# Two diagonal key steps of the softmax sums move from TensorE to VectorE, and the sum over keys moves three slots back

## The chip, the cores and the metric

The kernel runs on one core of a Trainium2 chip, as one launch. The metric is the device time of a run in microseconds (us). The cores that are not used do nothing. TensorE does the matmuls, ScalarE the exponentials and many copies out of PSUM, VectorE the row maxima and the small statistics, GpSimd long additions over SBUF tiles, SyncE issues the DMAs.

## What is computed

The input is two sequences of 2048 tokens with 1024 features. The layer is multi-query attention (32 heads of 32 features, one key and one value head) between two normalizations, and then a feed-forward of eight low-rank adapters mixed by a router, again between two normalizations, with a residual each time. Cut to what matters:

```python
q = (x @ wq).reshape(B, T, 32, 32); k = x @ wk; v = x @ wv
scores = einsum('bqhd,bkd->bhqk', q, k) * scale
scores = where(causal, scores, -inf)
out = einsum('bhqk,bkd->bqhd', softmax(scores), v).reshape(B, T, C) @ wo
x = x + layernorm(out)            # attention of layernorm(x)
x = x + layernorm(router_lora(layernorm(x)))
```

The change concerns the denominator of the softmax: for every query and head, the sum of the exponentials over all keys that the query may see.

## The kernel before

The queries are cut into blocks of 512 (four per sequence, eight in all), and each block into eight **units** of four heads. There are 64 units, n = 0 to 63; `n % 8` is the unit's place in its block, and the block's place in its sequence, `qb_of(n)`, says how many keys it sees. A unit goes over the keys in **steps** of 128: 4, 8, 12 or 16 steps for blocks 0 to 3. The last four steps of a unit lie on the diagonal: there only 512, 384, 256 and 128 of the queries see the keys, and the tiles are that wide. A **slot** is one head of one step, so a unit has 16, 32, 48 or 64 slots. Everything is set in order by slots: `pieces` (L139) lists, for each engine and each slot of a unit, the extra work that stands there, and every engine walks through the same slots in its own program.

In a slot TensorE computes the scores of one head and step (L1493, into a bank of PSUM), ScalarE takes their exponential into the tile `pr` (L834, one of three step buffers), and TensorE computes a block of scores for a later unit (L1481), of which VectorE takes the maximum over keys (L1086), so that the shift of the exponentials is known in time. The order in which scores and maxima take PSUM is one ring of five banks (L314, L1459): whoever comes next in TensorE's order takes the bank that was taken five places before, and waits until its reader is done. With one maximum per slot, the scores of slot j take the bank of the maximum of slot j-3.

When the four heads of a step are exponentiated, TensorE multiplies them with the values (L1517, four matmuls of 32 columns side by side, accumulated in one bank over the whole unit). This set stands a few slots later, beside the scores of the next step.

The **denominators** come together on two engines. For most steps GpSimd adds the four heads' tiles of the step to a running sum `ds` (L730: a step of full width is one instruction of 2048 elements per partition; the step 0 is added with step 1). At the end of a unit TensorE sums `ds` over the keys with a matmul by ones (`sum_keys`, L1557, in the list as "sums"). The steps that `by_pe` (L57) names are not added by GpSimd: TensorE multiplies their tiles by ones directly (L1542), right behind the values of that step, into the same bank that the sums then complete. In units of 12 steps these are the four diagonal steps 8 to 11, in units of 16 steps 12 to 15 (10 to 15 in the last two units of a block). GpSimd also masks the diagonal corner of each diagonal step (`mask`, L747).

After the sums ScalarE takes a first guess of the reciprocal (a logarithm and an exponential, "guess", L844), VectorE refines it in two operations (L1113) and scales the values with it (L1124). For units whose sums TensorE has begun itself, "sums" stands at slot 2 of the next unit, and the guess, the refinement and the scaling at slots 3 to 7. TensorE delays a piece to the next slot where the values stand and a projection is in front of it (`beside_values`, L200).

GpSimd's first addition of the next unit waits for the sums (`den_ready`), since it overwrites `ds`. An exponential that overwrites a step buffer waits for the values of three steps before and, where GpSimd adds that step, for its addition.

Beside this, the units carry the projections of other blocks, the residuals and the normalizations: VectorE's statistics of the attention's output (`att`, L1187), GpSimd's residual (L755: a scaling at L760 that needs VectorE's inverse root, and an addition at L762), GpSimd's normalization of the next block's tokens (L764) and its last residual sum of the layer (L769).

## Time and profile before

| | |
|---|---|
| median of 3 runs | 3328.93 us (3324.53 to 3332.82) |
| the profiled execution, its own time | 3326.88 us |
| its span, first to last instruction | 3325.1 us |
| TensorE busy | 96% |
| VectorE, GpSimd, ScalarE busy | 65%, 62%, 50% |
| mean granted TensorE clock | 0.986 |

The page of the profile gives shares of the span, the chain of work that ended last, and groups of instructions by line. Matmuls overlap, and their ends are modelled: the length of a set of matmuls is read from its start to the start of what follows it on TensorE, not from its own duration. A group "PEld" is the loading of weights, which runs beside the matmul before it; a load that waits costs time only where no matmul runs beside it. GpSimd is called POOL and VectorE DVE in the rows. Stretches are read from the table of windows, which gives each engine's busy time between two moments.

### The profile page before, as it was taken

Reading aid. Unit: us, or ns where it says so; the run is one execution under the profiler, and the core shown is the slowest. Engines: PE = TensorE matmul, PEld = TensorE weight load, DVE = VectorE, ACT = ScalarE, POOL = GpSimd, SP = SyncE. Lnnn points to the kernel's source line nnn. Section 1 sums busy time; section 2 is a strip of 40 time slices with the busy share of each in tenths; the row PEclk is TensorE's granted clock in tenths of the full one; section 3 lists DMA queues with packets and bytes.
Section 4 is the critical chain, followed back from the end, with each engine's and each line's share of the span. In section 5 each row is a group of like instructions: output and inputs, shape, how many; then the busy total and the mean of one; then the engine's idle time right before and its main releaser. Section 6 shows DMA issues by size and latency. Waiting matters only on the chain.

```text
span 3325.1 us, 45565 instructions
## 1 busy us (share of the span) xinstructions
PE 3191.2 (96%) x15976; PEld 1606.5 (48%) x15976; DVE 2163.1 (65%) x5848; ACT 1661.8 (50%) x3306; POOL 2061.2 (62%) x741
## 2 busy tenths in 40 slices
PE   7899999999999999999999999999999999999997
PEld 3444554455554455554444445544555444554444
DVE  4666677767767667774365667676776776677605
ACT  2334555555555555555433345545555554555552
POOL 1335676776676888777311176677576677778870
PEclk9999999999999999999999999999999999999998
DMA  4422111201101001101211211111010100011000
GB/s 118 116 61 65 52 52 39 61 26 30 52 23 58 23 23 30 29 23 39 64 52 52 81 45 40 42 44 60 26 56 23 39 17 23 26 43 48 7 1 26
DMA packets 133012, 144.04 MB, mean 43 GB/s; under 512 B 28200, under 2 KB 93736, under 8 KB 132784
## 3 DMA queue, kind: packets, MB, share of 16 engines
q1 hardware_dynamic: 132480, 140.72, 14.4%
q8 instruction: 127, 2.08, 0.3%
q14 instruction: 101, 0.83, 0.1%
q10 hardware_dynamic: 304, 0.41, 0.0%
HBM read 72.91 MB, written 16.78 MB: 27 GB/s over the span
## 4 chain that ended last, share of the span: by engine, by line
PE 73%; POOL 15%; DVE 5%; ACT 3%; issue 3%; SPq 1%; DMA 1%; POOLq 0%; ACTq 0%; DVEq 0%
PE ps L1501 14%; PE ps L1529 12%; PE ps L1490 12%; POOL ds L745 12%; PE ps L1632 11%; PE ps L1455 10%; PE ps L1542 3%; POOL ds L742 2%; PE ps L1591 2%; PE ps L1672 1%; ACT pr L842 1%; PE ps L1686 1%; PE ps L1564 1%; SPq L637 1%; PE ps L1642 1%
## 5 line engine op out<-in xcount | busy, mean ns | idle before, releaser
L842 ACT ACTIVATE pr<-ps 128x512 f32<-128x512 f32 (+3 forms) x2560 | 1299.8, 534 | 1303.0 <-PE ps L1501 885.0
L745 POOL TENSOR_TENSOR ds<-ds,pr 128x2048 f32<-128x2048 f32 (+1 forms) x360 | 1491.6, 4143 | 133.1 <-ACT pr L842 100.5
L1501 PE MATMUL ps<-qs,ks 98*128 98x512 f32 (+3 forms) x2560 | 1349.4, 534 | 22.4 <-ACT pr L842 6.7
L1095 DVE TENSOR_REDUCE mx<-ps 128x1 f32<-128x512 f32 x1536 | 1009.2, 685 | 389.7 <-PE ps L1490 381.7
L1490 PE MATMUL ps<-ks,qs 96*128 96x512 f32 (+3 forms) x2560 | 957.2, 385 | 51.6 <-ACT pr L842 28.8
L1501 PEld LDWEIGHTS ps<-qs,ks 98*128 98x128 f32 x2560 | 482.9, 190 | 763.7 <-issue 294.6
L1092 DVE CUSTOM_DVE_ANT_0 ps<-ps,mask_qk 128x128 f32<-128x128 f32 (+3 forms) x1024 | 498.4, 503 | 476.5 <-PE ps L1490 471.6
L1490 PEld LDWEIGHTS ps<-ks,qs 96*128 96x128 f32 x2560 | 486.7, 192 | 312.3 <-ACT pr L842 157.6
L1529 PE MATMUL ps<-pr,vs 128*32 128x512 f32 (+3 forms) x5120 | 612.0, 546 | 0.6 <-POOL pr L752 0.3
L1455 PE MATMUL ps<-xT,wq_sb 128*128 128x512 f32 x1024 | 513.7, 599 | 5.5 <-ACT zs L885 3.1
L1632 PE MATMUL ps<-wo_sb,ao 128*128 128x512 f32 x896 | 453.4, 598 | 0.5 <-DVE q L1084 0.5
L752 POOL TENSOR_SCALAR_AFFINE_SELECT pr<-pr 128x512 f32<-128x512 f32 x192 | 121.6, 634 | 464.6 <-ACT pr L842 464.6
L742 POOL TENSOR_TENSOR ds<-pr 128x2048 f32<-128x2048 f32 (+1 forms) x56 | 246.6, 4403 | 220.7 <-ACT pr L842 220.7
L1455 PEld LDWEIGHTS ps<-xT,wq_sb 128*128 128x128 f32 x1024 | 186.2, 192 | 82.6 <-issue 59.5
L1529 PEld LDWEIGHTS ps<-pr,vs 128*32 128x32 f32 x5120 | 102.8, 108 | 187.0 <-issue 155.6
L1632 PEld LDWEIGHTS ps<-wo_sb,ao 128*128 128x128 f32 x896 | 164.4, 191 | 57.7 <-issue 35.7
L1092 DVE DVE_READ_ACCUMULATOR2_ANT mx<- 128x1 f32 x1024 | 145.0, 142 | 0.0
L771 POOL TENSOR_TENSOR xr<-xr,zs 128x1024 f32<-128x1024 f32 x28 | 66.4, 2372 | 126.8 <-ACT zs L920 126.8
L1542 PE MATMUL ps<-pr,ones 128*32 128x512 f32 (+3 forms) x1344 | 129.8, 455 | 0.6 <-DVE ao L1127 0.6
L760 POOL TENSOR_SCALAR zs<-zs,r_att 128x1024 f32<-128x1024 f32 x28 | 31.2, 1114 | 131.4 <-DVE r_att L1049 131.4
L1084 DVE TENSOR_TENSOR q<-ps,q 128x512 fp32r<-128x512 f32 x64 | 44.2, 691 | 64.9 <-ACT q L826 64.9
L741 POOL COPY ds<-pr 128x512 f32<-128x512 f32 x8 | 4.9, 609 | 108.0 <-ACT pr L842 108.0
(166 smaller groups left out, 2105.7 us busy)
## 6 DMA issues: line engine op xcount, KB each, us to landing
qs<-q SPq DMA_DIRECT2D x762, 64.0 KB, 2.0
wq_sb<-in_L_attn_wq_dram SPq DMA_DIRECT2D x64, 512.0 KB, 4.0
t<-in_L_attn_x_dram SPq DMA_DIRECT2D x32, 512.0 KB, 6.3
xr<-in_L_attn_x_dram SPq DMA_DIRECT2D x28, 512.0 KB, 4.6
out_dram<-xr SPq DMA_DIRECT2D x28, 512.0 KB, 4.7
wo_sb<-in_L_attn_wo_dram SPq DMA_DIRECT2D x8, 512.0 KB, 5.2
qs<-mT SPq DMA_DIRECT2D x252, 4.0 KB
xT<-in_L_attn_x_dram SPq DMA_DIRECT2D x4, 512.0 KB, 5.5
```

The costliest lines, as they stand in the source:

```text
L742: nc.gpsimd.tensor_tensor(ds[:, :, c0:], first[:, :, c0:], this, ALU.add).then_inc(added, 1)
L745: nc.gpsimd.tensor_tensor(ds[:, :, c0:], ds[:, :, c0:], this, ALU.add).then_inc(added, 1)
L752: nc.gpsimd.affine_select(out=here, in_=here, compare_op=ALU.is_ge, fill=0.0, base=0, pattern=[[0, GH], [1, P]], channel_multiplier=-1).th ...
L842: nc.scalar.activation(pr[:, k % NS, g, c0:], ps[:, PM + EXP_PLACE[head(n, t, g)] % NPM, c0:], ACT.Exp, scale=SCALE).then_inc(exp_done, 1)
L1092: nc.vector.tensor_tensor_reduce(out=seen, in0=seen, in1=mask_qk[:, BLK - w:], op0=ALU.add, op1=ALU.max, scale=1.0, scalar=3.0 * NEG, accu ...
L1095: nc.vector.tensor_reduce(found, seen, AX.X, ALU.max).then_inc(mx_done, 1)
L1455: last = nc.tensor.matmul(ps[:, PX, :], wq_sb[:, n % NW, k, :], xT[:, k, :], start=(k == 0), stop=(k == KT - 1))
L1490: nc.tensor.matmul(ps[:, bank, 0:w], qs[0:STK, n % NS, g, qt * P:(qt + 1) * P], ks[0:STK, c:c + w], start=True, stop=True).then_inc(mx_rea ...
L1501: last = nc.tensor.matmul(ps[:, bank, c0:], ks[0:STK + 2, c:c + P], qs[0:STK + 2, n % NS, g, c0:], start=True, stop=not by_mask)
L1529: last = nc.tensor.matmul(ps[g * HD:(g + 1) * HD, PPV, c0:], vs[:, row, :], pr[:, (UNIT_STEP[n] + t) % NS, g, c0:], start=(t == 0), stop=( ...
L1542: last = nc.tensor.matmul(ps[g * HD:(g + 1) * HD, PAUX, c0:], ones[:, :], pr[:, (UNIT_STEP[n] + t) % NS, g, c0:], start=(t == by_pe(n)[0]) ...
L1632: last = nc.tensor.matmul(ps[:, PX, :], ao[:, (n + k) % NAO, j % TB * P:(j % TB + 1) * P], wo_sb[:, k, h * HALF:(h + 1) * HALF], start=(k ...
```

## The change

`by_pe` gives up the second and the third diagonal step in 30 units: in the sixteen of 12 steps (9 and 10, tiles of 384 and 256 columns) and in fourteen of the sixteen of 16 steps (13 and 14). The last unit of each sequence (n = 31 and 63) keeps what it had. A new function `hand_add` adds these steps on VectorE to GpSimd's running sum `ds`, one instruction per head, after GpSimd's last addition of the unit. A step's four adds stand two steps later in VectorE's program, one per slot behind that slot's maxima: for the first at the last four slots of the unit, for the second at slots 0 to 3 of the next. In these units the sums stand at slot 5 instead of 2, and the guess, the refinement and the scaling three slots later with them. ScalarE's exponential three steps on waits for the add of its head, and the sums wait for all adds of the unit.

```diff
     def by_pe(n):

+        if n % (NU * NQ) == NU * NQ - 1:
+            return (10, 11, 12, 13, 14, 15)
         if qb_of(n) == 3:
-            return (10, 11, 12, 13, 14, 15) if n % NU >= 6 else (12, 13, 14, 15)
-        return ((0, 1, 2, 3) if n >= NU else (), (), (8, 9, 10, 11), ())[qb_of(n)]
+            return (10, 11, 12, 15) if n % NU >= 6 else (12, 15)
+        return ((0, 1, 2, 3) if n >= NU else (), (), (8, 11), ())[qb_of(n)]
+
+    def by_dve(n):
+
+        return () if qb_of(n) < 2 or n % (NU * NQ) == NU * NQ - 1 else (TB * qb_of(n) + 1, TB * qb_of(n) + 2)
...
             if not whole(n - 1):
-                put(2 if by_pe(n - 1) else 6, "PE", "sums", n - 1)
-            first, apart = 3 if by_pe(n - 1) else 6 if N == 16 else 7, 2 if by_pe(n - 1) and N > 16 else 1
+                put(5 if by_dve(n - 1) else 2 if by_pe(n - 1) else 6, "PE", "sums", n - 1)
+            first, apart = 6 if by_dve(n - 1) else 3 if by_pe(n - 1) else 6 if N == 16 else 7, 2 if by_pe(n - 1) and N > 16 else 1
...
+        for m in range(max(n - 1, 0), n + 1):
+            for t in by_dve(m):
+                for g in range(GH):
+                    j = GH * (t + 2) + g - (slots(m) if m < n else 0)
+                    if 0 <= j < N:
+                        put(j, "DVE", "hand", m, t, g)
...
+                if k >= NS and step_of(k - NS)[1] in by_dve(step_of(k - NS)[0]):
+                    act.wait_ge(dve_added, hands_to(*step_of(k - NS), g))
                 act.wait_ge(st_ready, head(n, t, g) + 1)
...
+            def hand_add(n, t, g):
+
+                c0, _ = cols(n, t)
+                dve.wait_ge(added, UNIT_ADD[n + 1])
+                if t > by_dve(n)[0]:
+                    dve.wait_ge(dve_added, hands_to(n, t - 1, g))
+                dve.wait_ge(exp_done, head(n, t, g) + 1)
+                dve.wait_ge(masked, masks_to(n, t))
+                nc.vector.tensor_tensor(ds[:, g, c0:], ds[:, g, c0:], pr[:, (UNIT_STEP[n] + t) % NS, g, c0:],
+                                        ALU.add).then_inc(dve_added, 1)
...
             def sum_keys(n):
                 pe.wait_ge(added, UNIT_ADD[n + 1])
+                if by_dve(n):
+                    pe.wait_ge(dve_added, UNIT_HAND[n + 1])
```

How the instructions move is shown at the boundary from unit 26 to unit 27 (16 steps each). In these rows `ps<-qs,ks` are scores, `ps<-ks,qs` the blocks for the maxima, `pr,vs` values, `pr,ones` a step's sums on TensorE, `ds,ones` the sums over keys, `wo_sb,ao` projections. Line numbers of the changed kernel are higher, since lines were put in.

TensorE in the last slot of unit 26, before:

```order
L1490 MATMUL ps<-ks,qs 128x512
L1529 MATMUL ps<-pr,vs 32x256 x4
L1542 MATMUL ps<-pr,ones 32x256 x4
L1501 MATMUL ps<-qs,ks 128x512
L1490 MATMUL ps<-ks,qs 128x512
L1632 MATMUL ps<-wo_sb,ao 128x512
```

The same place in the change:

```order
L1524 MATMUL ps<-ks,qs 128x512
L1563 MATMUL ps<-pr,vs 32x256 x4
L1535 MATMUL ps<-qs,ks 128x512
L1524 MATMUL ps<-ks,qs 128x512
L1668 MATMUL ps<-wo_sb,ao 128x512
```

The set of step 14 is gone; the set of step 13 is gone in the same way four slots earlier.

TensorE from the values of the last step on, slots 2 and 3 of unit 27, before:

```order
L1529 MATMUL ps<-pr,vs 32x128 x4
L1542 MATMUL ps<-pr,ones 32x128 x4
L1501 MATMUL ps<-qs,ks 128x512
L1490 MATMUL ps<-ks,qs 128x512
L1632 MATMUL ps<-wo_sb,ao 128x512
L1564 MATMUL ps<-ds,ones 32x512 x4
```

In the change, from the projection of slot 3 on:

```order
L1668 MATMUL ps<-wo_sb,ao 128x512
L1535 MATMUL ps<-qs,ks 128x512
L1524 MATMUL ps<-ks,qs 128x512
L1535 MATMUL ps<-qs,ks 128x512
L1524 MATMUL ps<-ks,qs 128x512
L1563 MATMUL ps<-pr,vs 32x512 x4
L1535 MATMUL ps<-qs,ks 128x512
L1524 MATMUL ps<-ks,qs 128x512
L1668 MATMUL ps<-wo_sb,ao 128x512
L1600 MATMUL ps<-ds,ones 32x512 x4
```

The sums went from slot 3 to slot 6, each time behind a projection; the set of step 15 stays. In 16 of the 30 boundaries they end up at slot 6 like this, in the others at slot 5.

VectorE at the same boundary, slots 60 to 63 and 0, before (maxima are `mx<-ps`):

```order
L1048 TENSOR_SCALAR a_pre<-y_pre,w_pre 128x1
L1049 TENSOR_SCALAR r_pre<-a_pre,y_pre 128x1
L1148 TENSOR_SCALAR nb<-mv_pre,r_pre 128x1
L1095 TENSOR_REDUCE mx<-ps 128x1 x4
L1016 BN_STATS st_att<-zs 128x6
L1021 BN_AGGR mv_att<-st_att 128x2
L1095 TENSOR_REDUCE mx<-ps 128x1
```

In the change:

```order
L1180 TENSOR_SCALAR nb<-mv_pre,r_pre 128x1
L1142 TENSOR_TENSOR ds<-ds,pr 128x384
L1116 TENSOR_REDUCE mx<-ps 128x1
L1142 TENSOR_TENSOR ds<-ds,pr 128x384
L1116 TENSOR_REDUCE mx<-ps 128x1
L1142 TENSOR_TENSOR ds<-ds,pr 128x384
L1116 TENSOR_REDUCE mx<-ps 128x1
L1142 TENSOR_TENSOR ds<-ds,pr 128x384
L1116 TENSOR_REDUCE mx<-ps 128x1
L1037 BN_STATS st_att<-zs 128x6
L1042 BN_AGGR mv_att<-st_att 128x2
L1142 TENSOR_TENSOR ds<-ds,pr 128x256
```

Between each two maxima an add has come in; three more of 256 columns follow in slots 1 to 3, with the operations of the inverse root between them. GpSimd's and SyncE's programs keep their order.

## Rows read from the trace of the kernel before

**Rows 1.** The page: busy engines; the chain that ended last, by engine.
```profile
PE 3191.2 (96%) x15976; PEld 1606.5 (48%) x15976; DVE 2163.1 (65%) x5848; ACT 1661.8 (50%) x3306; POOL 2061.2 (62%) x741
...
PE 73%; POOL 15%; DVE 5%; ACT 3%; issue 3%; SPq 1%; DMA 1%; POOLq 0%; ACTq 0%; DVEq 0%
```

**Rows 2.** Windows: busy time of each engine at boundaries; the sum is over 28.
```profile
core 0: us, PE busy (x) PEld busy (x) DVE busy (x) ACT busy (x) POOL busy (x), PEclk, DMA share, GB/s
651.77:662.91 11.14, 11.05 (x78) 5.62 (x74) 7.17 (x15) 6.10 (x13) 1.82 (x2) 1.00 0.32 78
...
1268.70:1279.83 11.13, 11.13 (x79) 5.48 (x75) 8.65 (x24) 6.16 (x14) 4.30 (x4) 1.00 0.29 71
...
2758.78:2769.41 10.63, 10.54 (x77) 5.10 (x73) 6.53 (x11) 5.88 (x13) 0.63 (x1) 1.00 0.28 69
...
3054.14:3063.28 9.14, 9.14 (x74) 4.86 (x70) 7.39 (x18) 5.62 (x14) 2.99 (x2) 1.00 0.28 67
...
sum 306.18, PE 304.77 PEld 155.99 DVE 229.54 ACT 176.05 POOL 80.53; mean PE 10.88 PEld 5.57 DVE 8.20 ACT 6.29 POOL 2.88
...
1557.13:1573.13 16.00, 15.21 (x104) 6.57 (x100) 4.83 (x13) 11.50 (x25) 8.41 (x4) 1.00 0.32 83
```

**Rows 3.** Timeline of TensorE, boundary 26 to 27: start us, us, line, operation.
```profile
1267.94 0.83 PE L1542 MATMUL ps<-pr,ones 128*32 128x384 f32 x8
1268.70 0.33 PE L1501 MATMUL ps<-qs,ks 98*128 98x128 f32 x1
...
1271.57 0.61 PE L1542 MATMUL ps<-pr,ones 128*32 128x256 f32 x8
1272.12 0.50 PE L1501 MATMUL ps<-qs,ks 98*128 98x512 f32 x1
...
1275.74 1.02 PE L1632 MATMUL ps<-wo_sb,ao 128*128 128x512 f32 x2
1276.69 1.07 PE L1564 MATMUL ps<-ds,ones 128*32 128x512 f32 x8
1277.68 0.50 PE L1501 MATMUL ps<-qs,ks 98*128 98x512 f32 x1
```

**Rows 4.** Timeline of VectorE at the same boundary: maxima.
```profile
1269.34 0.69 DVE L1095 TENSOR_REDUCE mx<-ps 128x1 f32<-128x512 f32 x1 [1.27 <-PE ps L1490]
...
1270.63 1.88 DVE L1095 TENSOR_REDUCE mx<-ps 128x1 f32<-128x512 f32 x3
```

**Rows 5.** Whole span: waits of score loads (us, times, longest); idle of score matmuls.
```profile
PEld ps L1501 <- DVE mx L1095: 211.7, 352, 1.7
...
L1501 PE MATMUL ps<-qs,ks 98*128 98x512 f32 x1792 | 1001.7, 567 | 14.3 <-DMA qs<-mT 5.2 <-ACT pr L842 4.8 <-DVE mx L1095 2.3
```

**Rows 6.** VectorE: the add of two SBUF tiles (ns min/median/max); masked maxima by shape.
```profile
L1395 DVE TENSOR_TENSOR xT<-xT,t x6: 682/691/693, 3307.2 to 3321.8; 128x512 f32<-128x512 f32 x6
...
L1092 DVE CUSTOM_DVE_ANT_0 ps<-ps,mask_qk 128x512 f32<-128x512 f32 x256 | 177.1, 707 | 121.8 <-PE ps L1490 121.0
...
L1092 DVE CUSTOM_DVE_ANT_0 ps<-ps,mask_qk 128x384 f32<-128x384 f32 x256 | 141.7, 570 | 82.2 <-PE ps L1490 80.3
L1092 DVE CUSTOM_DVE_ANT_0 ps<-ps,mask_qk 128x256 f32<-128x256 f32 x256 | 108.5, 434 | 149.2 <-PE ps L1490 147.8
```

**Rows 7.** Timeline of GpSimd at the same boundary.
```profile
1260.55 4.55 POOL L745 TENSOR_TENSOR ds<-ds,pr 128x2048 f32<-128x2048 f32 x1
...
1271.44 0.63 POOL L752 TENSOR_SCALAR_AFFINE_SELECT pr<-pr 128x512 f32<-128x512 f32 x1 [3.21 <-ACT pr L842]
1272.06 1.19 POOL L766 TENSOR_SCALAR t<-t,r_pre,nb 128x1024 f32<-128x1024 f32 x1
1273.22 2.38 POOL L771 TENSOR_TENSOR xr<-xr,zs 128x1024 f32<-128x1024 f32 x1
1279.69 1.11 POOL L760 TENSOR_SCALAR zs<-zs,r_att 128x1024 f32<-128x1024 f32 x1 [4.09 <-DVE r_att L1049]
...
1283.21 4.57 POOL L742 TENSOR_TENSOR ds<-pr 128x2048 f32<-128x2048 f32 x1
```

More of the change, by code:

```diff
@@ L67, in adds_in, with by_gpsimd @@
     def adds_in(n, t):
-        return sum(x not in by_pe(n) for x in range(1, max(t, 1) + 1))
+        return sum(by_gpsimd(n, x) for x in range(1, max(t, 1) + 1))
+    def by_gpsimd(n, t):
+        return t not in by_pe(n) and t not in by_dve(n)
     UNIT_STEP = [0]
     UNIT_ADD = [0]
+    UNIT_HAND = [0]
     for n_ in range(UN):
         UNIT_STEP.append(UNIT_STEP[-1] + steps(n_))
+        UNIT_HAND.append(UNIT_HAND[-1] + GH * len(by_dve(n_)))
         UNIT_ADD.append(UNIT_ADD[-1] + adds_in(n_, steps(n_) - 1))
@@ L455, in bass_mqa_sandwich_lora_router @@
         off_ready = sem("off_ready")
+        dve_added = sem("dve_added")
         ao_ready = sem("ao_ready")
@@ L607, in masks_to, with hands_to @@
             return TB * (n - n // NU // NQ * NU - NU) + t - TB * qb_of(n) + 1
-        def by_gpsimd(n, t):
-            return t not in by_pe(n)
+        def hands_to(n, t, g):
+            return UNIT_HAND[n] + GH * by_dve(n).index(t) + g + 1
         def turn_bank(j, h):
@@ L1276, in _ @@
                     for stage, *a in at.get(j, []):
-                        if stage == "refine":
+                        if stage == "hand":
+                            hand_add(*a)
+                        elif stage == "refine":
                             refine(*a)
```

## Prediction

> **What bounds the kernel now.** I read the page first: TensorE is busy 96% of the span, and most of the chain that ended last is TensorE's own lines, with a part that passes through GpSimd's sums [rows 1]. So a matmul set taken from TensorE is worth its length, unless something else then ends last where it stood. The question is asked per unit boundary, because every removed set and every added VectorE instruction lies there: in the last four slots of a 12- or 16-step unit (44 to 47, or 60 to 63) and the first four of the next (0' to 3'). I call the stretch from the scores of the fourth-last slot to the scores of slot 6' a boundary; the change touches 30 of them (16 of 12-step units, 14 of 16-step units).
>
> The table of windows gives TensorE and VectorE there [rows 2]. TensorE is at full clock and busy for nearly all of each (304.77 of 306.18 us in 28 of them). VectorE is far from the 65% of the page: 8.65 of 11.13 us, 7.17 of 11.14, 7.39 of 9.14. Over the 28 it idles 306.18 - 229.54 = 76.64 us, 2.74 a boundary. Only behind the two units that are followed by little work for the maxima does it idle over 11 us (16.00 - 4.83 in one).
>
> The timelines of one boundary (26 to 27 of the first batch) show how the queues run [rows 3, 4]. What ties them is the ring of five banks: the scores of slot j take the bank that the maximum of slot j-3 left, where a slot has one maximum. So TensorE can be three slots ahead of VectorE, no more, and loads for scores do wait for a maximum, 211.7 us in 352 waits, nearly all of it behind a matmul that still streams: the matmuls themselves stood idle for it for 2.3 us [rows 5]. VectorE's chain starts 0.64 us behind the first scores (1268.70 to 1269.34), when the first maximum is there. Maxima in a row take 0.60 each (three in 1.88, one lasting 0.69).
>
> **What the change removes.** Two sets of ones-matmuls a boundary: 384 wide, 1267.94 to the next instruction at 1268.70, 0.76 us; 256 wide, 1271.57 to 1272.12, 0.55 us [rows 3]. That is 1.31 us, 39.3 us in 30. The sums of the keys (1276.69 to 1277.68) stay whole and move later; so do the two logarithm and exponential steps on ScalarE and the refinement and scaling on VectorE, without changing their work. They cost nothing by being later: the next user of that bank on TensorE is far down the unit. GpSimd's first addition of the next unit waits for the sums, but it needs the exponentials of slot 7' too, which come behind them; were the sums later than that, this addition would be next to be late.
>
> **What it adds.** Eight additions on VectorE a boundary, four of 384 and four of 256 columns, each reading both operands from SBUF. The one such instruction in the trace is 512 wide: 0.691 us [rows 6]. The masked maximum falls by 0.137 us with each 128 columns (0.707, 0.570, 0.434), so 0.555 and 0.418. Overlapped as maxima are (0.09), they hold the queue 0.46 and 0.33: 4 x 0.46 + 4 x 0.33 = 3.16 us a boundary. Their own waits, for GpSimd's last addition and for exponentials, are over by then: the addition ended at 1265.10 [rows 7], the first VectorE add comes after 1269. ScalarE's new wait, an exponential three steps on waiting for the add in its slot, ends before TensorE's: the maximum queued behind that add releases the scores three slots later.
>
> **The queue without collisions.** VectorE now has a continuous chain: 0.64 us start, all its work, the adds, and then the sums (1.0 us), during which it catches up with what was in the window behind slot 3'. The boundary then lasts its length less the idle time plus 3.16 + 0.64 = 3.80 us. With the 0.76 us saved ahead of it, a boundary changes by 3.04 us less its VectorE idle time: it breaks even at 3.04, and the mean is 2.74. For 28 boundaries: 28 x 3.04 - 76.64 = +8.5 us. In 16 of the 30 the sums come out at slot 6', behind a projection pair. There the scores of slot 6' wait for the maximum of slot 3' alone, not for the add (0.33) and small operations (up to 0.45) behind it, while the pair ahead of the sums costs 0.95 us where 0.46 is usual (1275.74 to 1276.69) [rows 3]; I credit 0.45 each, -7.2 us. The two with idle VectorE keep the whole saving, -2.6. Sum: -1.3 us. The queue gives back nearly all that TensorE gains.
>
> **Collisions with GpSimd.** In these slots GpSimd runs a mask (0.63 us), in 12 boundaries a normalization (1.19) and in 16 a residual sum (2.38) right behind it [rows 7]. All read SBUF, as both operands of the new adds do. What such an add does beside a running GpSimd instruction, the trace does not show: VectorE's instructions there read PSUM or one SBUF operand, and the adds of [rows 6] ran while GpSimd was idle. The lower end is nothing (0 us). The upper end is that an add waits until the running instruction has ended. An add comes about every 1.06 us (maximum 0.60, add 0.46), so it meets an instruction on average 0.53 us after its start: a residual sum costs 2.38 - 0.53 = 1.85, a normalization 0.66, a mask 0.63 x 0.63 / (2 x 1.06) = 0.19. In four 12-step boundaries the residual sum falls on some 1.3 us of statistics and small operations, and 0.55 is left. Sum: 12 x 1.85 + 4 x 0.55 + 12 x 0.66 + 28 x 0.19 = 37.6 us. In such a chain a wait is not made up: the maxima queue behind it, and TensorE is three slots from them. No row is near this case; that both operands come from the memory in which GpSimd's instruction works, while every VectorE instruction that ran beside GpSimd undisturbed had one there at most, makes me take the upper end, and keep both.
>
> The Trainium skill, page "SBUF — State Buffer", section "Who interferes with whom", says that a VectorE instruction with two SBUF inputs and a GpSimd instruction that reads SBUF shut each other out, the later one for the whole of the earlier. By that the sum is the upper end, without it the lower. No row of this trace shows it.
>
> **Sum.** The profiled execution took 3326.88 us (its span 3325.1), 2.05 below the median of the three runs. 3326.88 - 1.3 + 37.6 = 3363.2 us: **slower by 1.1%**.
>
> **Rivals.** (1) No collisions, the queue alone: 3326.88 - 1.3 = 3325.6, no change. For it: no row shows an instruction of either engine held up by the other. Its bounds: if every semaphore wait at the chain's end costs 0.3 us more, +9; if slots 4' to 6' take up half of the adds, -15. (2) The adds vanish in VectorE's idle time, because TensorE's lead of three slots (some 3 us) covers the whole of the 3.16 us and is rebuilt before the next boundary: then the removed sets count in full, 3326.88 - 39.3 = 3287.6, or about 3307 if half does. This is the other side. It decides where the idle time of a boundary is over 4.35 us (3.04 + 1.31); only 2 of 30 are, and 3 more come near (3.97 twice and 4.10 us [rows 2]), which speaks against it. (3) Collisions, and late statistics on top: the root that GpSimd's residual waits for (to 1279.69 [rows 7]) is behind the adds in VectorE's queue. In 10 boundaries the next unit's first GpSimd addition follows that residual at once, as at 1283.21; 1 us more in each gives 3373.
>
> **How the numbers follow.** About 0.3% (10 us) is what a measurement of this kernel can tell from no change. Collisions, with or without (3): 0.61, of it 0.58 slower by more than that and 0.03 where few adds meet an instruction. Rival 1: 0.24, of it 0.16 the same, 0.04 on either side. Rival 2: 0.15, of it 0.14 faster. That makes faster 0.18, same 0.20, slower 0.62. The range goes from 3314, which leaves out most of rival 2, to 3380 (rival 3 with some of the waits doubled); about 0.18 lies outside. The likeliest case alone has 3345 to 3380.
>
> **What would show it.** In the changed profile TensorE has 60 sets fewer (480 matmuls) and VectorE 240 adds. If I am right, TensorE's loads for scores wait more for VectorE, some adds last or wait until the end of a residual sum or normalization, and boundaries with a residual sum grow by 1.5 to 3 us while those with a mask alone stay within 1 us. If the adds run at 0.56 and 0.42 us straight through a residual sum, rival 1 is right. If boundaries shrink by 1.3 us each, rival 2 is. A chain that ends through GpSimd's first additions more than before speaks for rival 3. A change of more than 1 us outside the boundaries would show that I looked in the wrong place.

## The result and the profile after

The changed kernel takes 3403.98 us (3400.13 to 3408.60 in 4 runs), the kernel before, measured beside it, 3329.93. The ratio is 1.0223, with a 95% interval of 1.0209 to 1.0237. I forecast slower by 1.1% with a range of 3314 to 3380 us. The direction was right; the time is 40.8 us over my forecast and outside the range.

The profiled execution took 3408.60 us (span 3406.9), so the two profiled executions differ by 81.7 us. Busy engines and chain on the page of the changed kernel:

```profile
PE 3226.3 (95%) x15496; PEld 1607.5 (47%) x15496; DVE 2293.8 (67%) x6088; ACT 1667.3 (49%) x3306; POOL 2071.5 (61%) x741
...
PE 70%; POOL 13%; DVE 9%; issue 3%; ACT 3%; SPq 1%; DMA 1%; DVEq 0%; POOLq 0%; ACTq 0%
```

TensorE has the 480 matmuls fewer (15976 to 15496) and is nevertheless busy 35 us longer, 3226.3 against 3191.2 [rows 1]. Fewer instructions take longer together: either each waits inside, or the clock is lower. VectorE's part of the chain went from 5% to 9%, so the wait for VectorE is there too.

The table of windows tells the two apart. The windows run from the scores of the fourth-last slot to the scores of slot 8', not 6' as in [rows 2], since the sums now stand as late as slot 6'. Before, boundary 26 to 27 and the sum over the same 28 boundaries; every one of the 28 has a granted clock of 1.00 there:

```profile
1268.70:1282.19 13.49, 13.49 (x86) 6.94 (x83) 11.01 (x28) 7.33 (x16) 6.58 (x5) 1.00 0.40 103
...
sum 358.53, PE 356.95 PEld 190.78 DVE 278.79 ACT 206.56 POOL 111.50; mean PE 12.75 PEld 6.81 DVE 9.96 ACT 7.38 POOL 3.98
```

After, the boundaries behind units 17, 22, 26 and 29, and the sum:

```profile
712.66:728.77 16.11, 15.27 (x83) 7.31 (x79) 15.53 (x36) 7.08 (x15) 5.78 (x5) 1.00 0.40 114
...
1023.65:1039.41 15.76, 15.05 (x72) 7.98 (x69) 12.93 (x24) 5.73 (x12) 0.64 (x1) 0.68 0.32 83
...
1295.51:1314.01 18.50, 16.37 (x78) 7.71 (x75) 15.74 (x35) 7.22 (x16) 8.33 (x6) 0.82 0.39 108
...
1536.71:1553.55 16.84, 14.26 (x70) 6.87 (x67) 12.18 (x21) 6.18 (x14) 3.44 (x3) 0.70 0.38 110
...
sum 445.02, PE 399.64 PEld 193.13 DVE 392.86 ACT 193.38 POOL 128.53; mean PE 14.27 PEld 6.90 DVE 14.03 ACT 6.91 POOL 4.59
```

The 28 boundaries together grew by 86.5 us (445.02 - 358.53), so the place was right. The 384 wide set, which is gone, stood just ahead of these windows: from slot -8 to slot 14', which takes it in, the growth is 72.1 us of the 81.7. Part of the rest is in units 37 to 39, which the change leaves alone: together they are 3.8 us longer, with 17 us at the lower clock where the profile before has 3.4. Two things are new in the boundaries. TensorE stands idle 45.4 us (445.02 - 399.64), where it stood idle 1.6. And the granted clock, the figure behind the busy times, is below 1.00 in 12 of the 28. The sum of length x (1 - clock) over the 28 rows is 42.1 us; before it is 0. That is the most that the lower clock can have cost there, since in part of that time TensorE was waiting anyway. VectorE's idle time fell from 79.7 us (358.53 - 278.79) to 52.2 (445.02 - 392.86) though the boundaries became longer: behind unit 17 it is 0.58 of 16.11 us.

One boundary shows the sequence. These are VectorE, then GpSimd, at boundary 26 to 27 of the changed kernel (the place of [rows 4] and [rows 7]):

```profile
1298.51 0.78 DVE L1142 TENSOR_TENSOR ds<-ds,pr 128x384 f32<-128x384 f32 x1
...
1299.82 0.95 DVE L1142 TENSOR_TENSOR ds<-ds,pr 128x384 f32<-128x384 f32 x1
1300.69 0.68 DVE L1116 TENSOR_REDUCE mx<-ps 128x1 f32<-128x512 f32 x1
1301.30 2.11 DVE L1142 TENSOR_TENSOR ds<-ds,pr 128x384 f32<-128x384 f32 x1
1303.33 0.68 DVE L1116 TENSOR_REDUCE mx<-ps 128x1 f32<-128x512 f32 x1
...
1304.82 0.43 DVE L1142 TENSOR_TENSOR ds<-ds,pr 128x256 f32<-128x256 f32 x1
```

```profile
1298.25 0.64 POOL L771 TENSOR_SCALAR_AFFINE_SELECT pr<-pr 128x512 f32<-128x512 f32 x1 [2.56 <-ACT pr L863]
1298.88 1.49 POOL L785 TENSOR_SCALAR t<-t,r_pre,nb 128x1024 f32<-128x1024 f32 x1
1300.34 2.66 POOL L790 TENSOR_TENSOR xr<-xr,zs 128x1024 f32<-128x1024 f32 x1
```

The mask ends at 1298.89; the add that began beside it lasts 0.78 us where 0.55 is its undisturbed time. The next begins in the normalization and lasts to 0.4 us behind its end (1300.37). The third begins 0.96 us into the residual sum and lasts 2.11 us, to 0.4 us behind its end at 1303.00. The first add of 256 columns, with GpSimd idle, takes 0.43 us. GpSimd pays as well: the normalization takes 1.49 us where it took 1.19, the residual sum 2.66 where it took 2.38 [rows 7].

There is a kind of meeting that my forecast did not have, here behind unit 17 (VectorE, then GpSimd). The last add of 256 columns meets the scaling that opens GpSimd's residual, and takes 1.27 us:

```profile
725.31 1.27 DVE L1142 TENSOR_TENSOR ds<-ds,pr 128x256 f32<-128x256 f32 x1
```

```profile
725.20 1.12 POOL L779 TENSOR_SCALAR zs<-zs,r_att 128x1024 f32<-128x1024 f32 x1 [6.71 <-DVE r_att L1070]
```

This happens behind eight units (17 to 20 and 49 to 52).

TensorE there (the place of [rows 3]), and its granted clock in four stretches of the same boundary:

```profile
1301.43 0.50 PE L1535 MATMUL ps<-qs,ks 98*128 98x512 f32 x1 [0.64 <-DVE mx L1116]
...
1304.06 0.80 PE L1535 MATMUL ps<-qs,ks 98*128 98x512 f32 x1 [1.34 <-DVE mx L1116]
```

```profile
1295.51:1301.40 5.89, 5.12 (x28) 2.80 (x24) 5.19 (x12) 2.75 (x8) 3.33 (x4) 1.00 0.15 36
1301.40:1306.00 4.60, 3.24 (x22) 1.90 (x23) 4.53 (x8) 1.78 (x3) 1.59 (x1) 0.73 0.40 98
1306.00:1310.45 4.45, 4.45 (x14) 1.47 (x12) 4.29 (x14) 1.19 (x2) 0.00 (x0) 0.51 0.64 183
1310.45:1316.45 6.00, 6.00 (x32) 2.43 (x28) 3.52 (x7) 3.29 (x6) 5.66 (x3) 1.00 0.43 150
```

The scores wait for the maxima that queue behind the blocked adds. Then TensorE has work again and is busy for all of 1306.00 to 1310.45, but at 0.51, the lower of its two levels (1.2 GHz of 2.4): the blocked adds are over, and it still works at half speed. That is the part that my sum had no term for.

The waits, and then the groups by shape, of the whole span answer to [rows 5] and [rows 6]:

```profile
PEld ps L1535 <- DVE mx L1116: 247.7, 374, 2.9
```

```profile
L1535 PE MATMUL ps<-qs,ks 98*128 98x512 f32 x1792 | 1008.2, 571 | 45.3 <-DVE mx L1116 32.0 <-DMA qs<-mT 6.3 <-ACT pr L863 4.7
...
L1142 DVE TENSOR_TENSOR ds<-ds,pr 128x384 f32<-128x384 f32 x120 | 96.0, 804 | 23.1 <-POOL pr L771 23.1
...
L1142 DVE TENSOR_TENSOR ds<-ds,pr 128x256 f32<-128x256 f32 x120 | 57.3, 481 | 3.1 <-POOL pr L771 2.0 <-issue 0.7
```

The weight loads wait little more for maxima (247.7 against 211.7 us); it is the matmuls behind them that now stand idle for VectorE, 32.0 us against 2.3. That is the difference between a wait that is covered and one that is not. The adds are busy 96.0 + 57.3 = 153.3 us. By my undisturbed 0.555 and 0.418 they would be 120 x 0.973 = 116.8, so collisions made them 36.5 us longer. (The 23.1 us ahead of the wider ones are one wait for a mask, behind unit 62, where VectorE has little else to do.)

### The profile page after: what moved, and what is told of

It reads as the page before. It is cut to its first block, busy times and chain, and to the rows that moved or that the text cites. A ratio compares the mean times of both kernels' runs of the same rounds, so it can differ in the third digit from the quotient of the medians.

```text
span 3406.9 us, 45415 instructions
## 1 busy us (share of the span) xinstructions
PE 3226.3 (95%) x15496; PEld 1607.5 (47%) x15496; DVE 2293.8 (67%) x6088; ACT 1667.3 (49%) x3306; POOL 2071.5 (61%) x741
## 4 chain that ended last, share of the span: by engine, by line
PE 70%; POOL 13%; DVE 9%; issue 3%; ACT 3%; SPq 1%; DMA 1%; DVEq 0%; POOLq 0%; ACTq 0%
PE ps L1535 13%; PE ps L1563 12%; PE ps L1524 11%; PE ps L1489 10%; PE ps L1668 10%; POOL ds L764 10%; DVE mx L1116 3%; POOL ds L761 2%; DVE ds L1142 2%; PE ps L1627 2%; PE ps L1576 2%; ACT pr L863 2%; PE ps L1600 2%; PE ps L1708 2%; PE ps L1722 1%
## 5 line engine op out<-in xcount | busy, mean ns | idle before, releaser
L1524 PE MATMUL ps<-ks,qs 96*128 96x512 f32 (+3 forms) x2560 | 973.0, 392 | 65.5 <-ACT pr L863 30.6
L1524 PEld LDWEIGHTS ps<-ks,qs 96*128 96x128 f32 x2560 | 495.3, 196 | 326.3 <-ACT pr L863 153.5
L1563 PE MATMUL ps<-pr,vs 128*32 128x512 f32 (+3 forms) x5120 | 624.6, 556 | 1.1 <-POOL pr L771 0.7
L1142 DVE TENSOR_TENSOR ds<-ds,pr 128x384 f32<-128x384 f32 (+1 forms) x240 | 153.3, 642 | 26.2 <-POOL pr L771 25.1
L779 POOL TENSOR_SCALAR zs<-zs,r_att 128x1024 f32<-128x1024 f32 x28 | 31.3, 1119 | 171.0 <-DVE r_att L1070 171.0
L1576 PE MATMUL ps<-pr,ones 128*32 128x512 f32 (+3 forms) x864 | 89.2, 481 | 0.7 <-DVE ao L1159 0.7
```

The costliest lines, as they stand in the source:

```text
L1142: nc.vector.tensor_tensor(ds[:, g, c0:], ds[:, g, c0:], pr[:, (UNIT_STEP[n] + t) % NS, g, c0:], ALU.add).then_inc(dve_added, 1)
L1524: nc.tensor.matmul(ps[:, bank, 0:w], qs[0:STK, n % NS, g, qt * P:(qt + 1) * P], ks[0:STK, c:c + w], start=True, stop=True).then_inc(mx_rea ...
L1563: last = nc.tensor.matmul(ps[g * HD:(g + 1) * HD, PPV, c0:], vs[:, row, :], pr[:, (UNIT_STEP[n] + t) % NS, g, c0:], start=(t == 0), stop=( ...
L1576: last = nc.tensor.matmul(ps[g * HD:(g + 1) * HD, PAUX, c0:], ones[:, :], pr[:, (UNIT_STEP[n] + t) % NS, g, c0:], start=(t == by_pe(n)[0]) ...
```

## The experiments

Three theories stood at first. A: the adds wait out GpSimd's instructions, TensorE idles behind them, and then runs at its lower clock. B: collisions matter little, VectorE's queue is simply too full. C: the later sums hold something up. D and E are stated in the later expectations.

**The later sums alone.** The kernel before, with nothing but the sums, the guess, the refinement and the scaling moved as in the change:

```diff
+    def late(n):
+        return qb_of(n) >= 2 and n % (NU * NQ) != NU * NQ - 1
...
-                put(2 if by_pe(n - 1) else 6, "PE", "sums", n - 1)
+                put(5 if late(n - 1) else 2 if by_pe(n - 1) else 6, "PE", "sums", n - 1)
```

> TensorE keeps all its sets of ones as in the kernel before; only the sums over keys, the guess, the refinement and the scaling move three slots back in the same 30 boundaries. Theory A (the adds wait out GpSimd's instructions that also work on SBUF, TensorE idles behind them and then runs at its lower clock): no change, 3325 to 3336 us. Theory B (VectorE's queue is too full with the adds, collisions matter little): no change either. Theory C (the later sums hold up GpSimd's first addition and the bank of the sums): 3355 us or more.

Measured: 3342.32 us, ratio 1.0041 (1.0028 to 1.0054). Between the two expectations: being late costs about 14 us by itself (9 to 18 by the interval). The two profiled executions differ by 13.8 us, and the boundaries hold a part of it: eight behind 12-step units grow by 0.3 us and two by 0.9, most others hardly; in all 4.9 us to slot 8' and 7.9 from slot -8 to slot 14', with the clock at 1.00 in all 28. Length x (1 - clock) of the whole span is 54.1 us against 47.3 before, all of it outside the boundaries; whether that comes of the edit, one profile can't tell. Two waits grew by some 14 us, both of weight loads for their turn ("issue"): those of the sums, and those of the scores. Before, and with the sums late:

```profile
PEld ps L1501 <- issue: 294.6, 897, 1.7
...
PEld ps L1564 <- issue: 17.5, 35, 0.8
```

```profile
PEld ps L1504 <- issue: 308.9, 924, 1.7
...
PEld ps L1567 <- issue: 31.7, 68, 0.8
```

Those of the sums double, 35 to 68, and grow by 14.2 us; those of the scores grow by 14.3. Such a wait costs time only where no matmul runs beside it, so neither is shown to be the cause. C is right with a small part, and what exactly the late sums hold up stays open.

**The same adds with one operand from SBUF.** In the changed kernel each add becomes a reduction of the same tile, which doesn't read `ds`. The denominators lack two steps in 30 units:

```diff
-                nc.vector.tensor_tensor(ds[:, g, c0:], ds[:, g, c0:], pr[:, (UNIT_STEP[n] + t) % NS, g, c0:],
-                                        ALU.add).then_inc(dve_added, 1)
+                nc.vector.tensor_reduce(spare[:, (t % 2) * GH + g:(t % 2) * GH + g + 1], pr[:, (UNIT_STEP[n] + t) % NS, g, c0:],
+                                        AX.X, ALU.add).then_inc(dve_added, 1)
```

> Each of the 240 adds becomes a row sum over the same 384 or 256 columns of the exponentials, written to a spare column: the same place in the queue, the same waits, but one operand from SBUF. The denominators lack two steps in 30 units, so this computes less than the layer. Theory A: no instruction waits for GpSimd, and the time falls to 3318 to 3345 us, with TensorE's mean clock back at 0.98 or more. Theory B: the queue is as full as with the adds, 3390 us or more. Theory C: 3390 or more.

Measured: 3360.69 us, ratio 1.0096 (1.0076 to 1.0116). The reductions, by line:

```profile
L1143 DVE TENSOR_REDUCE spare<-pr x240: 406/480/553, 650.2 to 3218.9; 128x1 f32<-128x384 f32 x60, 128x1 f32<-128x256 f32 x60
```

They fill VectorE's queue as undisturbed adds would (406 to 553 ns, none longer), so 43 us of the 74 are the collisions and what they bring. The time lies outside A's range and below B's: A has the larger part, but 33 us stay. They are two things. In the 21 boundaries whose clock is at 1.00, my queue formula (3.04 us less VectorE's idle time, no credit for late sums) gives +2.9 us, and from slot -8 to slot 14' they grew by 6.1. Behind 26, for instance, the formula gives 3.04 - (11.13 - 8.65) = 0.56, and 0.54 was measured; it is worst behind 21 and 53, 1.4 us too low. In the seven others the granted clock over slots -4 to 14' is 0.76 to 0.93, with no idle stretch longer than 0.92 us in front. This is behind unit 23, from slot -4 on; the longest of its idle stretches is 0.45 us:

```profile
1060.36:1066.27 5.91, 4.97 (x27) 2.55 (x24) 5.78 (x11) 2.19 (x6) 0.64 (x1) 1.00 0.18 44
1066.27:1073.10 6.83, 6.83 (x36) 3.26 (x40) 5.33 (x11) 2.98 (x5) 0.00 (x0) 0.50 0.51 131
```

In these seven the formula gives 5.6 us and 23.7 was measured. So a fall of the clock costs about 18.1 / 7 = 2.6 us, and collisions are not needed for one.

**GpSimd waits instead.** In the changed kernel GpSimd's normalization, residual sum and residual of the first slots wait until the adds are done:

```diff
+                            if n and by_dve(n - 1) and GH * t + g < 16:
+                                pool.wait_ge(dve_added, UNIT_HAND[n])
```

> The changed kernel, but GpSimd starts its normalization, its last residual sum and its attention residual of the first slots only when VectorE's adds of the unit before are done. Only the masks can still collide. Theory A: most of the loss goes, 3330 to 3355 us; what is left is the masks, and GpSimd's first addition that comes 2 to 4 us later in the boundaries with all three instructions. Theory B: 3395 us or more, since VectorE's queue holds the same instructions. Theory C: 3395 or more.

Measured: 3389.24 us, ratio 1.0187 (1.0165 to 1.0208). The adds, and GpSimd's two instructions that wait for them:

```profile
L1144 DVE TENSOR_TENSOR ds<-ds,pr x240: 408/484/985, 649.0 to 3250.0; 128x384 f32<-128x384 f32 x60, 128x256 f32<-128x256 f32 x60
...
  POOL t L785: 97.4, 12
  POOL xr L790: 73.6, 10
```

Without the meetings (masks stay, hence the 985) the kernel gains 15 us and no more, which is outside A's range and below B's. GpSimd now idles 171 us for the adds, its first addition of the next unit comes later, ScalarE waits for that (71.9 us in place of 33.9), and the clock is still below 1.00 in nine boundaries. This run trades one wait for another, so it does not price the collisions.

**Filling the idle time.** Eight matmuls that add zeros, ahead of the scores of two slots, behind 12 units:

```diff
+    FILL = {20: 2, 21: 2, 26: 3, 27: 3, 28: 1, 29: 2, 52: 2, 53: 2, 58: 2, 59: 2, 60: 2, 61: 2}
...
+                    if j in (FILL.get(n - 1), FILL.get(n - 1, -9) - 1):
+                        for _ in range(4):
+                            nc.tensor.matmul(ps[:, PAUX, :], mask_qk[:, 0:P], mask_qk[:, :], start=False, stop=False)
```

> The changed kernel, with eight short matmuls that add zeros to the bank of the sums (four ahead of the scores of one slot, four ahead of the next) in the 12 boundaries in which TensorE stood idle for about 2 us behind blocked adds. They take the place of the idle time and compute nothing. Theory D (it is the idle time of TensorE that brings the stretch at 1.2 GHz behind it, and this stretch is the part of the excess that my sum had no term for): the granted clock of these boundaries returns to 1.00, or nearly, the waits for VectorE stay, and the time falls to 3370 to 3392 us from 3404. Rival E (the lower clock comes from something else in the changed program, or costs nothing because TensorE waits anyway): 3400 to 3415, with the clock as low as before or with it back at 1.00 and nothing gained.

Measured: 3391.59 us, ratio 1.0182 (1.0167 to 1.0197): 12 us faster than the changed kernel, by doing more. Boundary 26 to 27, whose four stretches in the changed kernel stand above, and behind unit 29, now:

```profile
1285.33:1302.24 16.91, 15.50 (x86) 7.06 (x83) 15.69 (x35) 7.22 (x16) 6.72 (x6) 1.00 0.41 112
...
1522.43:1536.00 13.57, 12.27 (x78) 5.84 (x75) 12.01 (x21) 6.08 (x14) 3.45 (x3) 1.00 0.31 76
```

The clock is back at 1.00, and the boundaries take 16.91 and 13.57 us where they took 18.50 and 16.84. The adds are blocked as before. Not all were cured: the sum of length x (1 - clock) over the 28 is 20.4 us, from 42.1, and behind units 20 and 52, where the clock fell all the same, the filling only cost time (1.5 and 0.8 us). The gain is also smaller than the clock's figure: seven boundaries came back to 1.00 (behind 21, 26 to 29, 53 and 59), where length x (1 - clock) had been 21.8 us, and they became 11.9 us shorter, 1.7 each. Behind 28 the clock went from 0.90 to 1.00 and the boundary stayed at 16.6 us, as rival E had it (the lower clock costs nothing where TensorE waits anyway). The time is 0.4 us inside the slow end of D's range. D holds in the main: filling the idle time brought the clock back in most of these boundaries, and part of the lost time with it.

**Idle time alone.** The kernel before, with one long VectorE instruction behind 12 units:

```diff
+        if n - 1 in STALL:
+            put(0, "DVE", "stall")
...
+                        if stage == "stall":
+                            nc.vector.tensor_reduce(spare[:, 0:1], ones[:, None, :].to_broadcast([P, 112, HD]), AX.XY, ALU.add)
```

> The kernel before with one more VectorE instruction, a reduction of 3584 elements of a constant (about 3.8 us, one SBUF operand, result unused), at slot 0 behind the same 12 units; no set is removed and nothing else is changed. By the queue formula a boundary grows by 3.8 + 0.64 us less its idle time of VectorE (2.3 us there on the mean), about 2.1 us, 25 us in all. Theory D: TensorE stands idle for 1 to 3 us in each, its granted clock falls to about 0.8 to 0.95 in most of these boundaries as in the changed kernel, and the boundary costs 2 to 4 us more than the formula: 3375 to 3405 us. Rival E: the clock stays at 1.00, 3343 to 3362 us.

Measured: 3368.34 us, ratio 1.0116 (1.0101 to 1.0131). VectorE and TensorE behind unit 20:

```profile
897.53 3.88 DVE L1282 TENSOR_REDUCE spare<-ones 128x1 f32<-128x3584 f32 x1
```

```profile
902.06 0.80 PE L1496 MATMUL ps<-ks,qs 96*128 96x512 f32 x1 [2.50 <-DVE mx L1099]
902.65 0.63 PE L1507 MATMUL ps<-qs,ks 98*128 98x512 f32 x1
```

Windows behind units 20 and 21, from the idle time on:

```profile
899.06:902.65 3.59, 1.09 (x6) 0.69 (x3) 3.56 (x5) 1.09 (x2) 0.00 (x0) 0.87 0.43 105
902.65:907.51 4.86, 4.86 (x17) 1.75 (x15) 4.39 (x11) 2.20 (x4) 2.23 (x2) 0.50 0.63 216
...
965.15:968.01 2.86, 0.75 (x6) 0.30 (x2) 2.86 (x3) 1.09 (x2) 0.00 (x0) 1.00 0.31 75
968.01:970.27 2.26, 2.25 (x13) 0.76 (x13) 2.26 (x5) 1.60 (x3) 0.00 (x0) 1.00 0.46 113
```

The first stood idle for 2.50 us and then worked at 0.50; the second stood idle for 2.11 and came back at 1.00. The same stall, two prices: to slot 8' the boundary behind 20 grew by 5.63 us, the one behind 21 by 2.49. Over the 12: the four with an idle time of 2.5 to 2.9 us all fell and grew by 5.4 to 6.2; of four with 2.06 to 2.13 two fell (+3.9 and +4.1) and two didn't (+2.5); the four with 1.08 didn't (+1.5). Where the clock stayed, a boundary grew by its idle time and 0.4 us; where it fell, by its idle time and 1.9 to 3.5. So a fall costs 1.5 to 3.1 us. The program in which this happens has neither adds nor later sums. The time lies between the two ranges: E's clock of 1.00 is refuted, and D's time was too high, because only six of the 12 fell.

**One step, one slot earlier.** Of the two steps only the 384 wide one goes to VectorE, with the sums where they were:

```diff
-        return () if qb_of(n) < 2 or n % (NU * NQ) == NU * NQ - 1 else (TB * qb_of(n) + 1, TB * qb_of(n) + 2)
+        return () if qb_of(n) < 2 or n % (NU * NQ) == NU * NQ - 1 else (TB * qb_of(n) + 1,)
...
-                    j = GH * (t + 2) + g - (slots(m) if m < n else 0)
+                    j = GH * (t + 2) + g - 1 - (slots(m) if m < n else 0)
```

> The changed kernel with only the second diagonal step (384 columns) on VectorE, its four adds one slot earlier each (ending one slot ahead of the next unit), the third step on TensorE again, and the sums, the guess, the refinement and the scaling at the slots of the kernel before. If collisions with long GpSimd instructions, the later sums and the clock are what cost 74 us, they are nearly all gone here, since the residual sums come later than these adds. By the queue formula a boundary changes by 1.84 + 0.64 - 0.76 = 1.72 us less VectorE's idle time, and at best by -0.76: 3306 to 3320 us. Rival: VectorE's idle time can't be used so close to its place, or the masks collide instead: 3325 to 3345 us.

Measured: 3350.31 us, ratio 1.0061 (1.0044 to 1.0078), a miss. The slot in the list is not the moment on the engine. VectorE and GpSimd behind unit 29:

```profile
1509.43 0.73 DVE L1142 TENSOR_TENSOR ds<-ds,pr 128x384 f32<-128x384 f32 x1
1510.08 0.68 DVE L1116 TENSOR_REDUCE mx<-ps 128x1 f32<-128x512 f32 x1
1510.68 2.11 DVE L1142 TENSOR_TENSOR ds<-ds,pr 128x384 f32<-128x384 f32 x1
```

```profile
1509.71 2.66 POOL L790 TENSOR_TENSOR xr<-xr,zs 128x1024 f32<-128x1024 f32 x1
```

VectorE runs more than a slot behind its list here: the add of slot -2 began at 1510.68, when TensorE had passed slot 0' (1509.81). One add out of four meets the residual sum, 0.97 us after its start, and that one is enough: TensorE stands idle 1.91 us. Nine boundaries shrank by 0.6 to 0.7 us from slot -8 to slot 14' (behind 17 to 20, 49 to 52 and 57), some of them with a residual sum that came after the adds. The others did not, and not only for residual sums: behind 23, with a mask alone, the clock fell to 0.76 and the boundary grew by 3.1 us.

**Two slots earlier still.** The same with `g - 3` in place of `g - 1`:

> As the run with one step on VectorE, with its four adds two slots earlier still (slots -7 to -4, counted from the next unit's slot 0). There the fourth add stood right behind the start of the residual sum and lasted up to 2.1 us, with TensorE idle 1.9 us at slot 2' and the clock down in six boundaries, while boundaries without a residual sum shrank by about 0.65 us. If that meeting is the whole of what was lost, the boundaries with a residual sum shrink as the others do: 0.5 to 0.7 us each, 15 to 20 us in 30, clock at 1.00 nearly everywhere: 3308 to 3318 us, faster than before. Rival: something else of the added work costs there (the full queue, waits for the masks, whose corner comes just ahead of the adds): 3322 to 3345 us.

Measured: 3334.45 us, ratio 1.0021 (1.0010 to 1.0031). The adds, by line:

```profile
L1142 DVE TENSOR_TENSOR ds<-ds,pr x120: 541/548/593, 643.6 to 3183.7; 128x384 f32<-128x384 f32 x120
```

No add is disturbed any more, though a mask is, as here in the last slots of unit 29 (VectorE, then GpSimd):

```profile
1492.99 0.55 DVE L1142 TENSOR_TENSOR ds<-ds,pr 128x384 f32<-128x384 f32 x1
```

```profile
1493.11 0.93 POOL L771 TENSOR_SCALAR_AFFINE_SELECT pr<-pr 128x512 f32<-128x512 f32 x1 [2.57 <-ACT pr L863]
```

The add came first, and the mask takes 0.93 us in place of 0.63. Behind the units with residual sums the clock is at 1.00. But the time is no better than before, because other boundaries now fall. Windows to slot 8' behind units 22 and 29:

```profile
996.27:1010.79 14.52, 12.96 (x80) 6.86 (x77) 11.77 (x21) 6.50 (x15) 0.93 (x2) 0.88 0.34 89
...
1493.56:1503.93 10.37, 10.37 (x78) 5.60 (x75) 9.15 (x16) 6.92 (x17) 3.47 (x3) 1.00 0.24 60
```

Behind 22 TensorE idles 1.56 us (three times 0.5) and the clock goes to 0.88: +3.1 us. Behind 29 it is busy throughout. In the trace of before, VectorE's idle time in slots -8 to -1 is 1.43 us behind unit 22 and 3.25 behind 29. The four adds hold the queue for 4 x 0.46 = 1.84. Theory and rival were each right in their own boundaries.

**Both steps early.** The changed kernel with the 384 wide adds at slots -7 to -4, the 256 wide ones at -4 and -3, the sums in their old slots:

```diff
-                    j = GH * (t + 2) + g - (slots(m) if m < n else 0)
+                    j = (GH * (t + 2) + g - 3 if t == by_dve(m)[0] else GH * (t + 1) + g // 2) - (slots(m) if m < n else 0)
```

> The changed kernel with both steps on VectorE, but the adds earlier (the 384 wide ones at slots -7 to -4, the 256 wide ones two per slot at slots -4 and -3), and the sums, the guess, the refinement and the scaling at the slots of the kernel before. If only the meetings with long GpSimd instructions, the lateness of the sums and the clock made the change slow, this one gains the 1.31 us of both sets in boundaries where VectorE has the idle time: 3295 to 3320 us. Rival, by the queue formula: 3.16 us of adds in so few slots fill VectorE's queue, which runs late into the residual sums again, the last adds wait and the clock falls as in the changed kernel: 3335 to 3385 us.

Measured: 3399.16 us, ratio 1.0210 (1.0195 to 1.0225). The rival is right, and its time was still too low: eight adds in five slots overfill the queue, and the longest lasts 2.58 us again. With the sums back in their old slots the kernel is still as slow; since the adds moved too, the run doesn't price the sums.

**One step, where there is room.** As in the run with adds at slots -7 to -4, in 20 units only:

```diff
-        return () if qb_of(n) < 2 or n % (NU * NQ) == NU * NQ - 1 else (TB * qb_of(n) + 1,)
+        return (TB * qb_of(n) + 1,) if qb_of(n) >= 2 and n != 61 and (1 <= n % NU <= 5 or n == 62) else ()
```

> As the last run with one step on VectorE (adds at slots -7 to -4), but in 20 units alone: those in which the trace of before shows more than 1.8 us of idle time on VectorE in slots -8 to -1, which is what four adds hold of the queue (4 x 0.46), the two with 1.81 us left out; the other units keep the kernel before. Theory (the added time fits the idle time of those slots, or it comes back as TensorE's, with the clock on top): 20 boundaries x -0.6 us = -12 us, no clock below 1.00 in any boundary, 3313 to 3321 us, the first of these versions to beat the kernel before. Rival (the gain of a removed set is not kept to the end of the unit): 3325 to 3335 us.

Measured: 3318.07 us (3314.78 to 3321.78), ratio 0.9961 (0.9948 to 0.9975). This version is faster than the kernel before, by 0.4%, and its median is 86 us below the changed kernel's. The adds, and the wait of the score loads for maxima:

```profile
L1142 DVE TENSOR_TENSOR ds<-ds,pr x80: 542/548/571, 707.2 to 3177.3; 128x384 f32<-128x384 f32 x80
```

```profile
PEld ps L1535 <- DVE mx L1116: 208.8, 357, 0.9
```

No add is longer than 0.57 us, and the wait is that of before, 211.7 [rows 5], with its longest at 0.9 instead of 1.7. The clock is at 1.00 at all the boundaries. 20 x 0.6 us had been expected; 10.8 us were measured.

## Why the prediction was right and wrong

**What bounds, and where.** Right in the main: 72.1 of the 81.7 us lie at 28 boundaries (slot -8 to slot 14'), and VectorE's queue there, not its 65%, decides.

**The removed sets.** Right in kind: the boundaries that lose one set and get an undisturbed, covered add shrink by 0.4 to 0.9 us, mostly 0.6 to 0.7 (a set of 384 was put at 0.76).

**The later sums.** Wrong: "They cost nothing by being later". By themselves they cost 14 us, 7.9 of it at the boundaries. My credit of 7.2 us for the sums at slot 6' has to go too: even without it the queue formula gives less than the run with one operand measured in the boundaries at full clock (2.9 against 6.1 us over 21).

**The added queue.** Right on the mean, 3.04 us less VectorE's idle time; for a single boundary it is good to 0.6 us in 18 of the 21, and up to 1.4 us too low in the others. I let ScalarE's new wait for the adds end before TensorE's; it does wait for them, 10.7 us in ten waits, and no run shows what that costs.

**Collisions.** Right in mechanism, and the total is right partly by luck: I took the upper end, 37.6 us, from the phase of adds and residual sums, and the adds became 36.5 us longer. By what GpSimd ran beside them (each add less the 0.548 or 0.418 us that it takes undisturbed, 38.4 us in all), residual sums made 24.1 us, where I had 24.4, normalizations 5.5 (7.9) and masks 1.9 (5.3); 6.9 us come from the eight meetings with the scaling of the residual, which I had left out. Rival 1 (they run straight through) is excluded by the 2.11 us add beside the 2.66 us residual sum. The Trainium skill, page "SBUF — State Buffer", section "Who interferes with whom", had said that two SBUF inputs beside a GpSimd instruction that reads SBUF shut each other out, the later waiting for the whole of the earlier. By that rule, this trace agrees: the add ends 0.4 us behind the residual sum, and the reductions with one SBUF input (0.55 us at most) weren't held up. GpSimd's own instructions became longer too, 2.66 us in place of 2.38, which fits the same rule from the other side. The sign that I gave for masks failed, though: four of the six boundaries with a mask alone grew by 1.8 to 4.4 us (to slot 8') in place of less than 1, and no add there is longer than 0.83 us.

**The root for the residual.** Rival 3 exists (GpSimd waits 171.0 us for the root of `att`, 131.4 before); whether that is a cause or a consequence of the longer boundaries, no run separates.

**The step that failed** is the Sum: it adds the waits and stops there. It treats TensorE's idle time as worth its own length. In this kernel TensorE had been at full clock in all 28 boundaries of the windows before, and I carried that 1.00 over without a term. Once it has stood idle there, it often works on at 1.2 GHz for some microseconds. In the changed kernel this happens at 12 of the 28 boundaries within the windows. A fall cost 1.7 us each where the filling took it away, 1.5 to 3.1 in the stall alone and 2.6 in the run with one operand; 3.5 (42.1 / 12) is the most that it can be on the mean. At 1.7 to 3.5 us each, 12 falls cost 20 to 42 us. The sum that should have stood there, an estimate: queue with late sums 11.7 us (6.1 measured and 5.6 by the formula), where I had -1.3; collisions 36.5; clock 20 to 42: 68 to 90 us against 81.7 between the two profiled executions. The parts overlap (the collisions' is VectorE's time, not TensorE's), so the agreement is a rough one. My range failed for the same reason: all its cases shared the missing term. What the filled idle time and the stall alone show is that the term is real and that idle time brings it; what exactly decides between a fall and none (about 2.1 us did it behind two units and not behind two others) stays open.

**Rival 2** (the adds vanish in VectorE's idle time) was refused for the right reason, that too few boundaries have the room; with half of the load, placed where the room is, in 20 boundaries, it is what the last run does.

## What to carry to other kernels

In a kernel whose TensorE is dense, price a new wait as the idle time and the stretch at the lower clock behind it; here TensorE's idle time grew by 43.8 us (45.4 - 1.6), and the second cost 20 to 42. Before giving VectorE work with two SBUF operands, put GpSimd's timeline beside the slots in which it will really run, which may be a slot or more behind the list, since one add that meets a long instruction can spoil the boundary. Count idle time per boundary, not on the mean: the same edit was mostly worth -0.4 to -0.7 us with 1.8 us of room and up to +3 without.

## What was not expected of the hardware

That boundaries with no idle time of TensorE over 0.92 us show a fall as well (granted clock 0.76 to 0.93 in seven boundaries of the run with one operand), while a single idle time of 2.1 us did not bring one in two of four. That more work on TensorE made the kernel faster: 96 matmuls of zeros, 12 us. And that both sides of a meeting pay: a GpSimd mask of 0.63 us takes 0.93 beside an add of VectorE that came first.
